# A graph layer and mixture of experts on one core: three sheets for the front of the edge list instead of five, and a ring of 24 gathered tiles in layer 2

## The chip, the cores and the metric

The kernel runs on one core of a Trainium2 chip. The metric is device microseconds of the execution; lower is better. The core has a tensor engine (PE; PEld are its weight loads), a vector engine (DVE), a scalar engine (ACT), GpSimd (POOL) and a sync engine (SP), each with its own instruction stream, and 16 DMA engines.

## What is computed

12500 nodes have 256 features each (x), and 200000 edges (src, dst, weight) are sorted by dst; dst is drawn as 12500 * uniform^2, so low nodes have many more edges. The part that the change touches is `_hconv`, which runs twice:

```
def _hconv(x, src, dst, ew, w1, b1, w2, b2, g, b):
    h = relu(x @ w1 + b1)
    msg = ew[:, None] * h[src]
    agg = segment_sum(msg, dst, num_segments=x.shape[0])
    h = agg @ w2 + b2
    return relu(_bn(h, g, b))
...
x0 = _layernorm(x)
h = relu(_bn(_hconv(x0, layer 1 weights)))
h = _bn(_hconv(h, layer 2 weights))
x = x + relu(h + x0)
x = x + ffn(_layernorm(x))      # 8 experts, all of them for each node, with softmax gates
```

## The kernel before, in words

**Stages.** A prologue (0 to 174 us) makes h of layer 1 and, on DVE, index tables from the edge list. `aggregate(0)` follows (175 to about 1800 us), then batch norms and h1 of layer 2, `aggregate(1)` (1928 to about 3430), and then the last norms and the experts, up to the end of the span.

**Edges.** They are cut into 391 groups of 512, a group into four tiles of 128. There are two ways for a group.

*Gathered groups.* For each tile t POOL issues an indirect DMA (L1054) that fetches 128 rows of h, 1 KB each, by `src_col` into slot t % R of a ring G of R = 16 tiles. The ring has no memory of its own: it lies in buffers that other stages use (`wst`, `f_xr`, `f_u`), so the trace shows these names. PE multiplies the four tiles of a group with four one-hot tiles OH (edge by dst, made by DVE, L1306, a ring of 12 tiles) in 16 matmuls (L1138) into a PSUM tile (`ps` or `px`), and DVE adds this to agg (L1420). Before each tile's first matmul PE waits for that tile's landing, on one semaphore per ring slot (`g_ga0` to `g_ga15`). The last matmul of a group counts `g_mm`, and before it refills four slots POOL waits for the count of the group that used them, four groups back. OH of a group waits for `g_mm` of three groups back.

*Front groups.* The lowest dst have so many edges that the front is done densely. A sheet is a matrix from all source nodes to a few hundred dst columns, made of edges (`MADE`): DVE makes one-hot rows of a tile of edges (`hot_rows`, L1317), ACT their other factor (`lows`, L1203 to L1216), PE multiplies the two (`hot_products`, L1092, tiles hw, ah, al into px) and DVE adds the product to the sheet in the upper part of agg (L1339). A finished segment of a sheet goes to memory by ACT's queue (`front`, L1193) and its place is cleared (L1184, L1225). To use a sheet (`USED`), SP loads it back in blocks (`work<-front`, `work<-h`), and PE multiplies h by it in 98 units (L1106, four matmuls into `pf`, as wide as the sheet), one for each block of 128 source nodes; a DVE add per segment ends it (L1355). Layer 1 makes four sheets (378, 462, 290 and 330 columns; 124 groups) and uses them; layer 2 uses them again, and makes and uses a fifth (416 columns, 16 groups).

So layer 1 gathers 267 groups (1067 tiles; the last group is not full), and layer 2 251 (1003 tiles). Layer 1 runs 496 tiles of edge products and 392 units, layer 2 64 and 490.

**Order.** Nothing is scheduled at run time. A planner at the head of the build places the products, the units and the 25 chunks of z = agg @ w2 (split on ACT L1273, remainder on DVE L1365, PE L1115) behind given groups. In layer 1 products stand behind groups 0 to 188, units behind 30 to 253, z chunks behind 196 to 266; in layer 2 units behind 0 to 229, and z chunks behind 56 to 250, three of them behind group 244 alone. While products run, two of the PSUM tiles serve the gathered groups in turn, and after that four.

Of the kernel before, what the change touches and what calls it, by code (L numbers as in the profile page):

```python
def build(nc, a, out):
# [94 lines left out]
    def sem(name):  # L96
        return top.enter_context(nc.semaphore(name))
# [38 lines left out]
    W_LAST = [SHEET[made[-1]][1] for made in MADE]  # L136
    CLEARS = 4
    A_W = [NHG * HG * max(SHEET[i][1] for i in made) for made in MADE]
# [16 lines left out]
    with top:  # L155
# [581 lines left out]
        R, RO = 16, 12  # L737
        RG, ROG, AG = R // GT, RO // GT, 2
# [3 lines left out]
        ga = [sem(f"g_ga{i}") for i in range(R)]  # L742
# [14 lines left out]
        def gathered_value(layer, t):  # L757

            return 16 * (layer * len(range(t % R, NTL[0], R)) + t // R + 1)
# [158 lines left out]
        def aggregate(layer):  # L918
# [3 lines left out]
            with ExitStack() as s:  # L922
                G = ([w[:, k, :] for w in wst for k in range(KC)] + [xr[:, j, :] for j in range(TPC)]
                     + [u[:, k, i * C:(i + 1) * C] for k in range(KC) for i in range(CH // C)])
                assert len(G) == R
# [8 lines left out]
                def seg_cells(m):  # L934
# [3 lines left out]
                steps = sb(s, f"steps{layer}", [P, WIN_W])[:, :]  # L938

                made_g = range(HOT_G[layer][0], FGL[layer]) if layer else range(FGL[0])  # L940
                ew_parts = sb(s, f"ew_parts{layer}", [P, 2 * GT * len(made_g)])[:, :].rearrange("p (h j f) -> p h j f", h=2, j=GT)
# [6 lines left out]
                    sb(s, f"hw{layer}_{i}", [P, WIN_W], f32r)[:, :] for i in range(2)]  # L948
# [19 lines left out]
                bank_of = [q % 2 if q <= hot_q[layer][-1] else q % 4 for q in range(NQL[layer])]  # L968
# [35 lines left out]
                with nc.Block() as block:  # L1004
                    @block.sync
                    def _(g):
                        if layer == 0:
                            g.wait_ge(window_st, 16 * FB)
                        lo = HOT_G[layer][0] if layer else 0
                        n = GT * (FGL[layer] - lo)  # L1010
                        g.dma_start(window_row[:, 0:n], window_dram[lo:FGL[layer], :].rearrange("(o f) j -> o (f j)", o=1)).then_inc(
                            window_in, 16)
# [35 lines left out]
                    def _(g):  # L1048
                        def gather(t):
                            e = F0[layer] + t  # L1050
                            col = e % GT * TW + e // GT
                            if t % GT == 0 and t >= R:
                                g.wait_ge(g_mm, E0 + t // GT - RG + 1)
                            g.indirect_dma_start(G[t % R], None, h_dram[layer], bass.IndirectOffsetOnAxis(  # L1054
                                ap=src_col[:, col:col + 1], axis=0)).then_inc(ga[t % R], 16)

                        g.iota(steps, pattern=[[1, WIN_W]], base=0, channel_multiplier=0,
                               allow_small_or_imprecise_dtypes=True).then_inc(steps_set, 1)
# [20 lines left out]
                    def _(g):  # L1079
# [48 lines left out]
                        for q in range(NQ):  # L1128
# [3 lines left out]
                            elif q >= 2:  # L1132
                                g.wait_ge(hot_a, H0 + NHOT[layer])
                            for k in range(KC):
                                for t in tiles_of[q]:
                                    if k == 0:
                                        g.wait_ge(ga[t % R], gathered_value(layer, t))
                                    ins = g.matmul(pS[bank_of[q]][:, k, :], G[t % R][:, k * P:(k + 1) * P], OH[t % RO],  # L1138
# [38 lines left out]
                    def _(g):  # L1177
# [42 lines left out]
                        clear(0)  # L1220
                        g.wait_ge(ew_set, 2 * layer + 2)
                        lows(0)
# [3 lines left out]
                        clear(1)  # L1226
# [28 lines left out]
                        for m in (len(made) - 2, len(made) - 1):  # L1255
                            g.wait_ge(hot_f[m % 2], hot_f_value(layer, m))
# [1036 lines left out]
```

## Time and profile before

| | us |
|---|---|
| median of 3 runs | 5256.29 |
| lowest, highest | 5254.63, 5257.71 |
| profiled execution, span | 5228.2 |
| layer 1: first gather to last add | 175.3 to 1796.9 |
| layer 2: first gather to last add | 1928.7 to 3412.5 |

| engine | busy us | share |
|---|---|---|
| PE | 4623.3 | 88% |
| PEld | 3800.6 | 73% |
| DVE | 2688.7 | 51% |
| ACT | 2435.6 | 47% |
| POOL | 2110.6 | 40% |

The profiled execution's own time is given only as its span, from the first to the last instruction; the median is 28 us above it. Shares are over the whole span, in which the experts alone (from about 3430 us) take 1800 us without POOL; the aggregations have to be read by their own stretches. A row of the windows view gives, for a stretch, the busy us and count of each engine in the order PE, PEld, DVE, ACT, POOL, then the granted clock of PE as a share of full speed, the DMA engines' busy share and GB/s. A timeline row gives start, duration, engine, line, operation, tiles, count, and in brackets the idle time ahead of it and what ended it; "issue" is the engine's own pause, "remote" a count that came from elsewhere and that the profile can't put to an instruction.

### The profile page before, as it was taken

Reading aid. Unit: us, or ns where it says so; the run is one execution under the profiler, and the core shown is the slowest. Engines: PE = TensorE matmul, PEld = TensorE weight load, DVE = VectorE, ACT = ScalarE, POOL = GpSimd, SP = SyncE. Lnnn points to the kernel's source line nnn. Section 1 sums busy time; section 2 is a strip of 40 time slices with the busy share of each in tenths; the row PEclk is TensorE's granted clock in tenths of the full one; section 3 lists DMA queues with packets and bytes.
Section 4 is the critical chain, followed back from the end, with each engine's and each line's share of the span. In section 5 each row is a group of like instructions: output and inputs, shape, how many; then the busy total and the mean of one; then the engine's idle time right before and its main releaser. Section 6 shows DMA issues by size and latency. Waiting matters only on the chain. (4 is left out here: it accounts for less than half of the span.)

```text
span 5228.2 us, 71544 instructions
## 1 busy us (share of the span) xinstructions
PE 4623.3 (88%) x25508; PEld 3800.6 (73%) x25508; DVE 2688.7 (51%) x6606; ACT 2435.6 (47%) x4218; POOL 2110.6 (40%) x2284
## 2 busy tenths in 40 slices
PE   6778888888999579888988988649999999999999
PEld 5667777666677467776666666548888888888888
DVE  7666666566333464522222222366666666666665
ACT  4655556666211263300000000057777777777777
POOL 1466666566666456666666666630000000000000
PEclk9889999999999789999999999779999999999999
DMA  5467777566755247876666666431111111001110
GB/s 155 148 210 271 243 240 245 188 211 217 236 198 201 77 141 268 277 243 218 218 219 205 226 212 224 131 96 25 30 28 33 33 33 33 24 26 33 33 28 15
DMA packets 546618, 770.23 MB, mean 147 GB/s; under 512 B 149720, under 2 KB 441411, under 8 KB 546262
## 3 DMA queue, kind: packets, MB, share of 16 engines
q1 hardware_dynamic: 328176, 382.01, 21.7%
q0 software_dynamic: 100944, 273.96, 16.4%
q10 hardware_dynamic: 117142, 109.65, 6.5%
q8 instruction: 206, 3.38, 0.3%
q14 instruction: 150, 1.23, 0.1%
HBM read 605.58 MB, written 147.26 MB: 144 GB/s over the span
## 5 line engine op out<-in xcount | busy, mean ns | idle before, releaser
L1106 PE MATMUL pf<-work 128*128 128x330 f32 (+4 forms) x3528 | 1251.9, 491 | 63.3 <-DMA work<-front 31.3
L1054 POOL DMA_INDIRECT wst<-h,src_col x1040 | 1000.3, 962 | 541.9 <-issue 275.0
L1106 PEld LDWEIGHTS pf<-work 128*128 128x128 f32 x3528 | 661.0, 197 | 402.2 <-issue 220.1
L2096 DVE TENSOR_TENSOR f_hl<-f_hf,f_hh 128x1024 fp32r<-128x1024 f32 (+1 forms) x400 | 479.7, 1199 | 636.3 <-ACT f_hf L1959 636.0
L1952 ACT ACTIVATE f_hh<-f_p,f_sh,f_sc 128x512 fp32r<-128x512 f32 (+1 forms) x800 | 571.7, 768 | 395.9 <-PE f_p L2194 394.5
L1273 ACT ACTIVATE ah<-agg 128x1024 fp32r<-128x1024 f32 (+1 forms) x50 | 51.8, 1037 | 1464.2 <-DVE agg L1420 1086.6
L1138 PEld LDWEIGHTS ps<-oh,wst 128*128 128x128 f32 x4160 | 543.4, 203 | 144.5 <-issue 99.6
L1138 PE MATMUL ps<-oh,wst 128*128 128x128 f32 x4160 | 560.7, 288 | 88.6 <-issue 55.1
L1054 POOL DMA_INDIRECT f_xr<-h,src_col x518 | 497.7, 961 | 282.8 <-issue 134.0
L1054 POOL DMA_INDIRECT f_u<-h,src_col x512 | 491.1, 959 | 260.5 <-issue 136.7
L1959 ACT ACTIVATE f_hf<-f_p,f_sh,f_sc 128x512 f32<-128x512 f32 (+1 forms) x800 | 572.5, 775 | 0.0
L1420 DVE TENSOR_TENSOR agg<-agg,ps 128x68 f32 (+25 forms) x378 | 99.3, 263 | 918.7 <-remote 604.0
L1339 DVE TENSOR_TENSOR agg<-agg,px 128x686 f32 (+5 forms) x560 | 399.3, 713 | 259.4 <-remote 107.7
L1306 DVE TENSOR_SCALAR oh<-lane,rel_col,ew_col 128x36 f32<-128x36 f32 (+27 forms) x2070 | 510.6, 337 | 0.0
L1420 DVE TENSOR_TENSOR agg<-agg,px 128x140 f32 (+20 forms) x140 | 40.5, 289 | 561.5 <-remote 428.6
L2108 DVE SCALAR_TENSOR_TENSOR f_x<-f_p,f_gate,f_x 128x256 f32<-128x256 f32 x784 | 324.4, 476 | 2.4 <-PE f_p L2249 2.4
L2249 PE MATMUL f_p<-Wo_hi,f_hh 128*128 128x256 f32 (+1 forms) x1568 | 317.4, 284 | 2.4 <-DVE f_x L2108 2.4
L2249 PE MATMUL f_p<-Wo_lo,f_hh 128*128 128x256 f32 (+1 forms) x1568 | 314.4, 282 | 0.0
L2249 PE MATMUL f_p<-Wo_hi,f_hl 128*128 128x256 f32 (+1 forms) x1568 | 314.2, 282 | 0.0
L2249 PEld LDWEIGHTS f_p<-Wo_hi,f_hh 128*128 128x128 f32 (+1 forms) x1568 | 250.8, 189 | 25.9 <-issue 11.1
L2194 PE MATMUL f_p<-f_hh,W_hi 128*128 128x512 f32 (+1 forms) x800 | 252.9, 397 | 1.2 <-ACT f_hf L1959 1.2
L2194 PE MATMUL f_p<-f_yh,W_hi 128*128 128x512 f32 (+1 forms) x800 | 248.1, 391 | 4.4 <-DVE f_yl L2047 2.4
(285 smaller groups left out, 7648.0 us busy)
## 6 DMA issues: line engine op xcount, KB each, us to landing
work<-h SPq DMA_DIRECT2D x216, 512.0 KB
work<-front SPq DMA_DIRECT2D x50, 924.0 KB
front<-agg ACTq DMA_DIRECT2D x12, 3300.0 KB
work<-front SPq DMA_DIRECT2D x50, 756.0 KB
work<-front SPq DMA_DIRECT2D x50, 660.0 KB
work<-front SPq DMA_DIRECT2D x50, 580.0 KB
front<-agg ACTq DMA_DIRECT2D x8, 2600.0 KB
work<-front SPq DMA_DIRECT2D x25, 832.0 KB
```

What stands on the lines that cost most here:

```text
L1054: g.indirect_dma_start(G[t % R], None, h_dram[layer], bass.IndirectOffsetOnAxis(ap=src_col[:, col:col + 1], axis=0)).then_inc(ga[t % R], 16)
L1106: ins = g.matmul(pF[:, k, 0:count * w].rearrange("p (s c) -> p s c", c=w), HB[a % 2][0:r, n, k * P:(k + 1) * P], x, start=b == 0, stop=b = ...
L1138: ins = g.matmul(pS[bank_of[q]][:, k, :], G[t % R][:, k * P:(k + 1) * P], OH[t % RO], start=t == tiles_of[q][0], stop=t == tiles_of[q][-1])
L1306: ins = g.tensor_scalar(OH[t % RO][:, 0:wide], lane[:, 0:wide], rel_col[:, col:col + 1], ew_col[:, col:col + 1], ALU.is_equal, ALU.mult)
L1339: g.tensor_tensor(v, v, x, ALU.add).then_inc(hot_a, 1)
L1420: g.tensor_tensor(win, win, pS[bank_of[q]][:, :, 0:wide], ALU.add).then_inc(g_add, 1)
L1952: ins = g.activation(hhi[l][q % 2][:, m, 0:nn], p[:, m, 0:nn], ACT.Relu, bias=shift[l][:, col], scale=scale[l][:, col])
L1959: ins = g.activation(hf[l][:, m, 0:nn], p[:, m, 0:nn], ACT.Relu, bias=shift[l][:, col], scale=scale[l][:, col])
L2096: g.tensor_tensor(hlo[l][q % 2][:, :, 0:nn], hf[l][:, :, 0:nn], hhi[l][q % 2][:, :, 0:nn].bitcast(fp32), ALU.subtract).then_inc(f_lo[l], 1)
L2108: ins = g.scalar_tensor_tensor(X1[0:r, j, :], p3[0:r, j, :], gate[c % 2][0:r, j, e:e + 1], X1[0:r, j, :], ALU.mult, ALU.add)
L2194: ins = g.matmul(o[:, m, 0:nn], ww[:, k, m * P:(m + 1) * P], xx[:, k, 0:nn], start=i == 0 and k == 0, stop=i == 2 and k == KC - 1)
L2249: ins = g.matmul(p3[0:r, j, :], x[:, k, j * P:j * P + r], w[:, k, :], start=n == 0 and k == 0, stop=n == 2 and k == KC - 1)
```

## The change

The front has three sheets instead of five: 378 and 462 columns as before, and a third of 290 columns with 14 groups. Both layers use the same three, 108 groups in all. Layer 1 makes them, layer 2 makes nothing. So 283 groups (1131 tiles) are gathered in both layers; products are 432 tiles in layer 1 (behind groups 0 to 172) and none in layer 2, units 294 in each. With 108 front groups instead of 140, their index tables fit one block of 128 (`FB` is 1 instead of 2). `WIN_W`, the width of the one-hot rows and of the iota ahead of layer 2's gathers, goes from 784 to 688; layer 2 has neither. Its ring gets 8 tiles of memory of their own (`ring1`) behind the 16, so POOL waits for the group six back; layer 1 keeps 16. A semaphore `g_ga` now counts the landings of a group's four tiles together, and PE waits for the four once, ahead of the group's 16 matmuls. In layer 2 four PSUM tiles serve the gathered groups from the start. Units stand behind groups 31 to 268 and z chunks behind 180 to 282 in layer 1, units behind 0 to 226 and z chunks behind 52 to 282 in layer 2, with no three of them behind one group there.

```diff
-               (58, [(5, 3, 7)]),
-               (66, [(5, 3, 7)]),
-               (52, [(2, 2, 7), (6, 2, 8)])]
-    MADE = [[3, 2, 1, 0], [4]]
-    USED = [[3, 2, 1, 0], [3, 2, 1, 0, 4]]
+               (58, [(4, 3, 7), (1, 2, 7)]),
+               ]
+    MADE = [[2, 1, 0], []]
+    USED = [[2, 1, 0], [2, 1, 0]]
...
-    FRONT_C = [3, 4]
+    FRONT_C = [3, 3]
...
-    HOT_Q = [188, 48]
+    HOT_Q = [172, 0]
...
-        R, RO = 16, 12
-        RG, ROG, AG = R // GT, RO // GT, 2
+        R, RO = [16, 24], 12
+        ROG, AG = RO // GT, 2
...
-        ga = [sem(f"g_ga{i}") for i in range(R)]
+        RG = [r // GT for r in R]
+        ga = [sem(f"g_ga{i}") for i in range(max(RG))]
...
-                assert len(G) == R
+                if R[layer] > len(G):
+                    more = sb(s, f"ring{layer}", [P, R[layer] - len(G), C])
+                    G += [more[:, i, :] for i in range(R[layer] - len(G))]
+                ring = R[layer]
...
-                steps = sb(s, f"steps{layer}", [P, WIN_W])[:, :]
+                steps = sb(s, f"steps{layer}", [P, WIN_W])[:, :] if made else None
...
-                bank_of = [q % 2 if q <= hot_q[layer][-1] else q % 4 for q in range(NQL[layer])]
+                bank_of = [q % 2 if made and q <= hot_q[layer][-1] else q % 4 for q in range(NQL[layer])]
...
-                            if t % GT == 0 and t >= R:
-                                g.wait_ge(g_mm, E0 + t // GT - RG + 1)
-                            g.indirect_dma_start(G[t % R], None, h_dram[layer], bass.IndirectOffsetOnAxis(
-                                ap=src_col[:, col:col + 1], axis=0)).then_inc(ga[t % R], 16)
+                            if t % GT == 0 and t >= ring:
+                                g.wait_ge(g_mm, E0 + (t - ring) // GT + 1)
+                            g.indirect_dma_start(G[t % ring], None, h_dram[layer], bass.IndirectOffsetOnAxis(
+                                ap=src_col[:, col:col + 1], axis=0)).then_inc(ga[t // GT % RG[layer]], 16)
...
+                            g.wait_ge(ga[q % RG[layer]], gathered_value(layer, q))
                             for k in range(KC):
                                 for t in tiles_of[q]:
-                                    if k == 0:
-                                        g.wait_ge(ga[t % R], gathered_value(layer, t))
```

POOL, the start of layer 2. Before, an iota stands ahead, and the first wait for `g_mm` comes behind 16 gathers:

```order
L1047 UNCONDITIONAL_BRANCH [waits barrier_Pool_Activation_PE_DVE_SP_gather]
L1057 IOTA steps1 128x784
L1054 DMA wst<-h1,src_col 128x256 x8
L1054 DMA f_xr<-h1,src_col 128x256 x4
L1054 DMA f_u<-h1,src_col 128x256 x4
L1054 DMA wst<-h1,src_col 128x256 [waits g_mm]
L1054 DMA wst<-h1,src_col 128x256 x3
```

The same place after the change:

```order
L1057 UNCONDITIONAL_BRANCH [waits barrier_Pool_Activation_PE_DVE_SP_gather]
L1064 DMA wst<-h1,src_col 128x256 x8
L1064 DMA f_xr<-h1,src_col 128x256 x4
L1064 DMA f_u<-h1,src_col 128x256 x4
L1064 DMA ring1<-h1,src_col 128x256 x8
L1064 DMA wst<-h1,src_col 128x256 [waits g_mm]
L1064 DMA wst<-h1,src_col 128x256 x3
```

Eight more gathers stand ahead of the first wait, and the iota is gone.

PE, layer 1, gathered group 60, before: its matmuls (L1138), then edge products (L1092) and a unit (L1106) of the 330-column sheet:

```order
L1138 MATMUL ps0_0<-oh0,wst 128x128 [waits g_ga0,g_add,g_oh]
L1138 MATMUL ps0_0<-oh0,wst 128x128 [waits g_ga1]
L1138 MATMUL ps0_0<-oh0,wst 128x128 [waits g_ga2]
L1138 MATMUL ps0_0<-oh0,wst 128x128 [waits g_ga3]
L1138 MATMUL ps0_0<-oh0,wst 128x128 x4
L1092 MATMUL px0_1<-ah0_0,ah0_1 128x294 [waits hot_a,hot_m]
L1092 MATMUL px0_1<-ah0_0,ah0_1 128x294 x3
L1106 MATMUL pf0<-work0 128x330 [waits batch_in1]
L1106 MATMUL pf0<-work0 128x330
```

The same group after the change:

```order
L1148 MATMUL ps0_0<-oh0,wst 128x128 [waits g_ga0,g_add,g_oh]
L1148 MATMUL ps0_0<-oh0,wst 128x128 x7
L1103 MATMUL px0_1<-hw0_1,al0 128x294 [waits hot_a,hot_m]
L1103 MATMUL px0_1<-hw0_1,al0 128x294 x3
L1117 MATMUL pf0<-work0 128x290 x2
L1103 MATMUL px0_0<-ah0_0,al0 128x294 [waits hot_a,hot_m]
L1103 MATMUL px0_0<-ah0_0,al0 128x294 x3
```

Four waits for landings became one, and the units are those of the 290-column sheet.

PE, layer 2, gathered group 100, before, with units of the 462-column sheet behind it:

```order
L1138 MATMUL ps1_0<-oh1,wst 128x128 [waits g_ga0,g_add,g_oh]
L1138 MATMUL ps1_0<-oh1,wst 128x128 [waits g_ga1]
L1138 MATMUL ps1_0<-oh1,wst 128x128 [waits g_ga2]
L1138 MATMUL ps1_0<-oh1,wst 128x128 [waits g_ga3]
L1138 MATMUL ps1_0<-oh1,wst 128x128 x4
L1106 MATMUL pf1<-work1 128x462 [waits batch_in1]
L1106 MATMUL pf1<-work1 128x462 x3
```

The same group and the next after the change:

```order
L1148 MATMUL ps1_0<-oh1,ring1 128x128 [waits g_ga4,g_add,g_oh]
L1148 MATMUL ps1_0<-oh1,ring1 128x128 x7
L1117 MATMUL pf1<-work1 128x462 x2
L1148 MATMUL ps1_1<-oh1,ring1 128x128 [waits g_ga5,g_add,g_oh]
L1148 MATMUL ps1_1<-oh1,ring1 128x128 x7
L1117 MATMUL pf1<-work1 128x462 x2
```

Half as many unit matmuls stand between two gathered groups, and the group reads the new tiles of the ring.

## Rows read from the trace of the kernel before

**Rows 1.** Windows: us, PE, PEld, DVE, ACT, POOL busy, clock, DMA share; both aggregations.

```profile
175.00:1338.00 1163.00, 974.52 (x5537) 814.00 (x5538) 726.03 (x1945) 706.98 (x1689) 740.38 (x765) 0.93 0.67 222
1338.00:1779.00 441.00, 396.94 (x2004) 298.59 (x2003) 150.45 (x486) 50.55 (x47) 291.53 (x303) 0.95 0.57 192
1928.00:2243.00 315.00, 274.57 (x1496) 227.75 (x1496) 150.35 (x394) 108.11 (x216) 204.81 (x213) 0.93 0.77 258
2243.00:3397.00 1154.00, 1002.41 (x4926) 737.61 (x4924) 292.70 (x1095) 51.73 (x46) 751.06 (x791) 0.92 0.62 211
```

**Rows 2.** Timeline of POOL in layer 2, about 3300 us.

```profile
3299.36 0.95 POOL L1054 DMA_INDIRECT wst<-h,src_col  x1 [0.30 <-issue]
3303.01 0.95 POOL L1054 DMA_INDIRECT f_xr<-h,src_col  x1 [2.70 <-remote]
```

**Rows 3.** Idle time of POOL ahead of gathers (us, times), layer 1, then layer 2.

```profile
  remote: 174.9, 97
  PE ps L1138: 119.4, 70
...
  issue: 272.2, 892
  remote: 195.6, 90
  PE ps L1138: 28.2, 15
```

**Rows 4.** Timelines of POOL and DVE: iota, last gather and last add of each layer.

```profile
1779.00 0.95 POOL L1054 DMA_INDIRECT f_xr<-h,src_col  x1 [0.30 <-issue]
1796.59 0.33 DVE L1420 TENSOR_TENSOR agg<-agg,px 128x164 f32 x1 [1.01 <-PE px L1138]
1927.80 0.79 POOL L1057 IOTA steps<- 128x784 f32 x1 [9.48 <-POOLq L1570]
1928.74 1.01 POOL L1054 DMA_INDIRECT wst<-h,src_col  x1 [0.16 <-issue]
3396.96 0.95 POOL L1054 DMA_INDIRECT f_xr<-h,src_col  x1 [0.30 <-issue]
3412.15 0.32 DVE L1420 TENSOR_TENSOR agg<-agg,px 128x164 f32 x1 [1.01 <-PE px L1138]
```

**Rows 5.** The page's first line.

```profile
span 5228.2 us, 71544 instructions
```

**Rows 6.** Prologue: the window from 40 to 80 us, and a DVE group by form.

```profile
40.00:80.00 40.00, 22.43 (x106) 19.19 (x107) 36.33 (x148) 14.57 (x26) 0.00 (x0) 0.76 0.35 106
L568 DVE TENSOR_TENSOR agg<-agg,window_f 128x1024 f32<-128x1024 f32 x1 | 1.2, 1219 | 0.0
```

**Rows 7.** Timeline of PE: edge products, a unit of 330, a gathered group, units of 462.

```profile
443.36 0.88 PE L1092 MATMUL px<-hw,ah 128*128 128x344 f32 x4
444.08 1.27 PE L1106 MATMUL pf<-work 128*128 128x330 f32 x4
...
2559.08 3.27 PE L1106 MATMUL pf<-work 128*128 128x462 f32 x8
2562.19 1.95 PE L1138 MATMUL ps<-oh,wst 128*128 128x128 f32 x16
```

**Rows 8.** Timeline of PE at the end of layer 2: z chunks behind group 244.

```profile
3390.88 1.22 PE L1115 MATMUL px<-ah,w_hi 128*128 128x512 f32 x2 [10.77 <-DVE al L1365]
```

**Rows 9.** Windows again: L1106 alone, then all engines in stretches of different load.

```profile
234.00:354.00 120.00, 0.00 (x0) 0.00 (x0) 0.87 0.60 196
...
234.00:354.00 120.00, 86.05 (x505) 77.50 (x504) 76.68 (x187) 73.05 (x154) 78.78 (x82) 0.87 0.60 196
614.00:734.00 120.00, 105.88 (x645) 91.41 (x644) 77.68 (x198) 69.32 (x166) 78.74 (x80) 0.96 0.71 235
1698.00:1758.00 60.00, 50.03 (x274) 40.95 (x273) 19.55 (x69) 3.94 (x4) 40.22 (x43) 0.89 0.42 131
1758.00:1779.00 21.00, 10.51 (x63) 9.06 (x61) 7.39 (x24) 4.26 (x5) 13.35 (x16) 0.76 0.30 89
3290.00:3350.00 60.00, 38.42 (x203) 32.96 (x202) 19.37 (x66) 3.94 (x4) 39.02 (x42) 0.74 0.36 109
```

More of the change, by code:

```diff
@@ L755, in build, with gathered_value, landed @@
         z_out = sem("z_out")
-        def gathered_value(layer, t):
-            return 16 * (layer * len(range(t % R, NTL[0], R)) + t // R + 1)
+        def gathered_value(layer, q):
+            def landed(n, x):
+                return 16 * min(GT, NTL[n] - x * GT)
+            slot = q % RG[layer]
+            before = sum(landed(0, x) for x in range(slot, NQL[0], RG[0])) if layer and slot < RG[0] else 0
+            return before + sum(landed(layer, x) for x in range(slot, q + 1, RG[layer]))
         NFL = [NHG * len(used) for used in USED]
@@ L947, in aggregate @@
                 HW = [AH[0][:, :, :].rearrange("p k n -> p (k n)")[:, 0:WIN_W]] + [
-                    sb(s, f"hw{layer}_{i}", [P, WIN_W], f32r)[:, :] for i in range(2)]
+                    sb(s, f"hw{layer}_{i}", [P, WIN_W], f32r)[:, :] for i in range(2) if made]
                 RH = len(HW)
@@ L1008, in _ @@
                             g.wait_ge(window_st, 16 * FB)
[L1009 to L1012, printed above, removed]
+                        if made:
+                            lo = HOT_G[layer][0] if layer else 0
+                            n = GT * (FGL[layer] - lo)
+                            g.dma_start(window_row[:, 0:n], window_dram[lo:FGL[layer], :].rearrange(
+                                "(o f) j -> o (f j)", o=1)).then_inc(window_in, 16)
                         def load(a):
@@ L1218, in lows @@
                             ins.then_inc(hot_l, 1)
-                        clear(0)
-                        g.wait_ge(ew_set, 2 * layer + 2)
-                        lows(0)
+                        if made:
+                            clear(0)
+                            g.wait_ge(ew_set, 2 * layer + 2)
+                            lows(0)
                         if layer == 0:
@@ L1225, in _ @@
                                 g.activation(agg[:, k, 0:UPPER[0]], zero_col[:, :].broadcast_to([P, UPPER[0]]), ACT.Copy).then_inc(agg_set, 1)
-                        clear(1)
+                        if made:
+                            clear(1)
                         ends = [seg_end(layer, m) for m in range(len(made))]
@@ L1253, in _ @@
                                 store(m)
-                        for m in (len(made) - 2, len(made) - 1):
-                            g.wait_ge(hot_f[m % 2], hot_f_value(layer, m))
-                        g.wait_ge(hot_p, H0 + NHOT[layer])
-                        for k in range(KC):
-                            g.activation(upper[k][:, free_w:], zero_col[:, :].broadcast_to([P, A_W[layer] - free_w]),
-                                         ACT.Copy).then_inc(agg_set, 1)
+                        if made:
+                            for m in (len(made) - 2, len(made) - 1):
+                                g.wait_ge(hot_f[m % 2], hot_f_value(layer, m))
+                            g.wait_ge(hot_p, H0 + NHOT[layer])
+                            for k in range(KC):
+                                g.activation(upper[k][:, free_w:], zero_col[:, :].broadcast_to([P, A_W[layer] - free_w]),
+                                             ACT.Copy).then_inc(agg_set, 1)
                         def split(n):
```

40 lines of the change are left out of this document (22 added, 18 removed).

## The prediction

> **What bounds the kernel now.** I read the stages first: busy time of every engine in four stretches that cover the two aggregations [rows 1]. In none of them is an engine full. TensorE is busy 975 of 1163 us, 397 of 441, 275 of 315 and 1002 of 1154 (84, 90, 87 and 87%); GpSimd, which only gathers, 64 to 66%. But GpSimd's busy time leaves out its issue time. One gather is 0.95 us and then 0.30 us of issue [rows 2], so by the counts of [rows 1] the floor of a group of four tiles is 4 x 1.25 = 5.0 us, and the pace that was reached is 1163 / (765 / 4) = 6.08, 441 / (303 / 4) = 5.82 and, in layer 2, 1469 / 251 = 5.85 us. The rest is waiting, and the second view says for what: GpSimd sat idle for matmuls (remote, and PE ps) for 174.9 + 119.4 us in layer 1 and 195.6 + 28.2 us in layer 2 [rows 3]. Taking off the 0.30 us that each of these 272 gaps would have had anyway leaves about 244 and 192 us. The timeline shows the form: eight gathers back to back, then 2.70 us until a group's matmuls have given its ring slots back [rows 2]. So an aggregation is bound by a loop of gather, landing, matmul, and the ring of 16 tiles (four groups) that closes it, between two engines that are both nearly loaded: GpSimd at 5.0 us a group and TensorE, from [rows 1], at (975 + 397) / 267 = 5.14 in layer 1 and (275 + 1002) / 251 = 5.09 in layer 2. Everything after 3412 us (the last add [rows 4]) and the 130 us between the layers is untouched.
>
> **What the change moves, priced.** The base is the profiled execution, span 5228.2 us [rows 5]; the median of 5256.3 lies 28 us above it, and I add that to the end of every sum, since nothing of the change touches it.
>
> *Prologue.* 108 front groups fit one block of 128 instead of two, so the index work on 128x1024 tiles halves: of five operations at 1.2 us (one is in [rows 6]) half is 3.0 us, and two at 0.7 us, three pairs at 2 x 0.74, 2 x 0.48 and 2 x 0.48 us and small ones bring about 2.8 more, 5.8 us in all. It is on the path in part: VectorE is busy 36.3 of 40 us there [rows 6]. Lost copies, stores and their landings go with it. Taken: -7 us, between -2 and -10.
>
> *TensorE, layer 1.* The removed sheet of 330 columns takes 98 units at 1.27 us = 124 us, and 64 tiles of edge products at 0.72 us (444.08 less 443.36) = 46 us [rows 7]; 16 more gathered groups at 1.95 us cost 31. Net -139: (1372 - 139) / 283 = 4.36 us a group instead of 5.14.
>
> *TensorE, layer 2.* Two sheets leave. The 330 one is 124 us again; the 416 one lies between 330 and 462 columns (1.27 and 3.27 / 2 = 1.64 us), say 1.5, x 98 = 147. Its 64 tiles of products are 46, 32 more groups cost 62. Net -255: (1277 - 255) / 283 = 3.61 us a group. VectorE and ScalarE lose the making too (busy 150 and 108 us of the first 315 [rows 1]); it lay beside GpSimd's work and is worth nothing by itself.
>
> *GpSimd.* Layer 1 has 16 groups more, layer 2 has 32: at the floor 16 x 5.0 = 80 and 160 us of new work on the engine that is now nearest to its own limit.
>
> *Layer 2, ring of 24.* The wait is now for the group six back. The first wait comes at gather 25 instead of 17, and in steady state a slot may be away for 6 x 5.0 = 30 us where 4 x 5.85 = 23.4 us are used now, which is the whole round with its waits in it. TensorE at 3.61 us has room. So I take the floor: 1131 gathers at (204.8 + 751.1) / 1004 + 272.2 / 892 = 0.952 + 0.305 = 1.257 us [rows 1, 3] = 1422 us, plus 10 for leftover waits, plus 16 from last gather to last add (3396.96 to 3412.15 [rows 4]) = 1448, against 3412.5 - 1928.7 = 1484 now: -36. The iota before the first gather (0.79 us [rows 4]) goes: -1. The pile-up at the end, where TensorE waits up to 10.77 us for VectorE's part of three z chunks [rows 8], no longer stands there; no gather waited for it, so it is worth 0. Bounds: -46 (no leftover) and, if the ring gives nothing, 283 x 5.85 + 16 = 1672, +188.
>
> *Layer 1, same ring of 16.* This term decides. At today's paces it would be 172 x 6.08 + 111 x 5.82 + 18 = 1710 us against 1622 (175 to the last add at 1797; 18 is from last gather to last add [rows 4]): +88. At the floor, 1131 x 1.257 + 18 = 1440: -182. What does the pace do when TensorE has less to do? Three rows bear on it [rows 9]. From 234 to 354 us no unit ran (0.00 in the row of L1106), and 82 gathers went out: 5.85 us a group, against 80 (6.0) from 614 to 734 with TensorE 88% busy. From 1698 to 1758, TensorE at 83%, 43 gathers: 5.58; from 1758 to 1779, at 50%, 16 gathers: 5.25. I take 5.9 for the 172 groups beside products (nearest to the unit-free 5.85, since a third of the units is gone) and 5.55 for the 111 behind (nearest to 5.58, the same ring at about the load that all of them will have): 1015 + 616 + 18 = 1649, +27 us.
>
> *Landings per four tiles.* In front of a group's 16 matmuls stands one wait instead of four. It delays the first matmul to the last tile's landing, at most the few matmuls of the first three tiles (under 0.5 us of the 1.95), in the loop of layer 1 only; fewer semaphore instructions stand against it. Taken 0, between -3 and +15 us over layer 1.
>
> *Sum.* -7 + 27 - 36 - 1 = -17: span 5211, time 5239 us, 0.3% faster. It is a small difference of large terms: all but layer 1 brings -44, so the sign turns where layer 1 runs at (1622 + 44 - 18) / 283 = 5.82 us a group over all; today's mean is 6.01, my forecast 5.76.
>
> **Rules of the skill.** On landing: what the rows show is that a slot's round takes 23.4 us in layer 2. The Trainium skill, DMA: Bandwidth & Descriptors, section on the anatomy of one DMA, puts one gather of 128 KB at about 2.0 us plus its bytes over 436 GB/s, so 2.3 us; by that estimate a round is 5.0 + 2.3 + 1.95 = 9.3 us, a ring of 16 would never wait, and the larger ring would be worth nothing. The 224 us of waits decide against it here: most of the round is time behind other work in TensorE's queue and on the way back of the count.
>
> **Rivals.**
> (a) Slower: layer 1's pace stays. For: with no units at all the pace was 5.85, only 0.2 better; from 3290 to 3350 us TensorE was busy 64% and the pace 60 / (42 / 4) = 5.7 [rows 9], so the round of the 16-tile ring looks like latency that an emptier TensorE does not shorten. Against: 5.58 and 5.25 at the end of layer 1. Price: +88 instead of +27, total +44: 5300 us. It decides from 5.82 us a group.
> (b) Slower: layer 2 does not reach GpSimd's floor. The clock is 0.96 while TensorE is 88% busy and 0.74 where it is 64% busy [rows 9]; an emptier TensorE would do its 3.61 us at that clock in 3.61 / 0.74 = 4.9, and with waits the pace could be 5.5: 283 x 5.5 + 16 = 1572, +124 on my layer 2: about 5363. The Trainium skill, TensorE: Matmul & The Clock Gate, Part 1, has the same as a rule: an engine that was idle runs at half clock. The trace agrees (0.74 as a mean of the two levels); the price above is from the rows.
> (c) Faster: two engines near their limits hold each other up, and with TensorE at 4.36 layer 1 follows GpSimd: 283 x 5.4 + 18 = 1546, -76, total -120: 5136 at the end, 5165 at 5.5. For: 5.25 in the last 21 us. Against: 5.85 without units, where TensorE waited for VectorE's adds instead.
>
> **How the numbers follow.** A measurement of this kernel tells 0.2%, 10.5 us, from no change. My forecast 0.46, with its own range 5211 to 5267 from the paces 5.8 to 6.0 and 5.45 to 5.65: 0.32 faster, 0.11 same, 0.03 slower. (a) 0.32: 0.05 same, 0.27 slower. (b) 0.10 slower. (c) 0.12 faster. Together faster 0.44, same 0.16, slower 0.40. The range leaves out the lower half of (c), a little of (a) and most of (b): 5165 to 5312.
>
> **What the profile after would show.** Right: last gather of layer 2 some 1430 us after its first, GpSimd's gaps there 0.30 us almost throughout and no remote idle; layer 1's first 172 groups in about 1015 us and its last 111 in 616; first gather at 168 instead of 175. Wrong on layer 1: 1047 and 646 us with the same remote idle per group as before (0.9 us). Wrong on layer 2: remote idle over 50 us, or clock under 0.8 with TensorE's gather matmuls longer. The forecast falls if layer 1 runs above 5.82 us a group.

## The result: 4.2% slower, and where the time went

The changed kernel takes 5476.32 us (median of 4 runs, 5467.4 to 5482.1) where the kernel before takes 5255.46 us (median of 4 runs, 5250.6 to 5257.7); the ratio is 1.0418, 95% interval 1.0404 to 1.0433. The forecast was 5239 us with a range of 5165 to 5312: wrong in sign, and the result lies 164 us above the range.

Both profiled executions, step by step (a gather's start is the time in its row):

| | before, us | after, us | change |
|---|---|---|---|
| start to layer 1's first gather | 175.3 | 166.4 | -8.9 |
| layer 1, first to last gather | 1603.7 (1067) | 1697.3 (1131) | +93.6 |
| to layer 2's first gather | 149.7 | 140.6 | -9.1 |
| layer 2, first to last gather | 1468.3 (1003) | 1645.1 (1131) | +176.8 |
| to the end of the span | 1831.2 | 1824.3 | -6.9 |
| span | 5228.2 | 5473.7 | +245.5 |

All of the loss lies in the two gathering stretches. The windows of the profile after answer to [rows 1]; the first is layer 1's 172 groups with products, the second its last 111, the third layer 2:

```profile
166.00:1218.00 1052.00, 809.09 (x4558) 687.33 (x4558) 609.48 (x1710) 601.64 (x1459) 669.06 (x690) 0.90 0.59 188
1218.00:1864.00 646.00, 532.63 (x2589) 399.16 (x2587) 199.11 (x670) 55.76 (x61) 420.92 (x443) 0.88 0.51 164
2004.00:3649.00 1645.00, 1243.43 (x5932) 954.93 (x5932) 388.23 (x1515) 45.01 (x46) 1073.47 (x1130) 0.81 0.49 156
```

TensorE's share fell, from 84 to 77% in the first, from 90 to 82% in the second, from 87 to 76% in layer 2, though less than reckoned: it was busy (809 + 533) / 283 = 4.74 and 1243 / 283 = 4.39 us a group, where the prediction had 4.36 and 3.61. The pace did not follow at all: 1052 / 172 = 6.12, 646 / 111 = 5.82 and 1645 / 283 = 5.81 us a group, against 6.08, 5.82 and 5.85 before. Each group that left the sheets was paid at nearly the full old pace: 16 groups in layer 1 cost 94 us (5.85 each), 32 in layer 2 cost 177 us (5.5 each). GpSimd's waits in layer 1, and then in layer 2 with its ring of 24:

```profile
its engine sat idle before it (us, times) until:
  issue: 299.2, 978
  remote: 213.3, 109
  PE ps L1148: 84.2, 39
...
  issue: 318.3, 1036
  remote: 228.9, 83
  PE ps L1148: 14.1, 7
```

Against [rows 3], the waits for matmuls are as long as ever: 298 us in layer 1 instead of 294, 243 in layer 2 instead of 224. In layer 2 only their form changed: between two waits GpSimd now mostly runs twelve gathers (before, eight or twelve), with 96 gaps over 0.5 us instead of 106. The run with a ring of 16 below has 97 such gaps, so even that is not the ring's doing. What held GpSimd was not the ring's length.

### The profile page after: what moved, and what is told of

The parts are those of the page before. It is cut to its first block and busy times, and to the rows that moved or that the text cites. A ratio compares the mean times of both kernels' runs of the same rounds, so it can differ in the third digit from the quotient of the medians.

```text
span 5473.7 us, 68832 instructions
## 1 busy us (share of the span) xinstructions
PE 4546.6 (83%) x24573; PEld 3753.0 (69%) x24573; DVE 2553.6 (47%) x6561; ACT 2216.6 (40%) x3779; POOL 2285.9 (42%) x2471
## 5 line engine op out<-in xcount | busy, mean ns | idle before, releaser
L1064 POOL DMA_INDIRECT wst<-h,src_col x947 | 907.6, 958 | 521.6 <-issue 252.7
L1117 PE MATMUL pf<-work 128*128 128x290 f32 (+2 forms) x2352 | 960.6, 536 | 77.3 <-issue 73.3
L1117 PEld LDWEIGHTS pf<-work 128*128 128x128 f32 x2352 | 467.0, 213 | 326.4 <-issue 242.7
L1435 DVE TENSOR_TENSOR agg<-agg,ps 128x52 f32 (+27 forms) x370 | 95.6, 258 | 1060.4 <-remote 736.2
L1148 PE MATMUL ps<-oh,wst 128*128 128x128 f32 x3040 | 454.7, 301 | 145.3 <-issue 108.9
L1148 PEld LDWEIGHTS ps<-oh,wst 128*128 128x128 f32 x3040 | 431.4, 215 | 194.2 <-issue 177.1
L1319 DVE TENSOR_SCALAR oh<-lane,rel_col,ew_col 128x30 f32<-128x30 f32 (+28 forms) x2262 | 562.5, 338 | 0.2
L1435 DVE TENSOR_TENSOR agg<-agg,px 128x124 f32 (+28 forms) x196 | 53.9, 275 | 898.7 <-remote 713.0
L1064 POOL DMA_INDIRECT ring<-h,src_col x376 | 358.3, 953 | 202.7 <-issue 106.3
L1352 DVE TENSOR_TENSOR agg<-agg,px 128x294 f32 (+4 forms) x432 | 283.3, 656 | 180.0 <-remote 99.3
```

The costliest lines, as they stand in the source:

```text
L1064: g.indirect_dma_start(G[t % ring], None, h_dram[layer], bass.IndirectOffsetOnAxis(ap=src_col[:, col:col + 1], axis=0)).then_inc(ga[t // G ...
L1117: ins = g.matmul(pF[:, k, 0:count * w].rearrange("p (s c) -> p s c", c=w), HB[a % 2][0:r, n, k * P:(k + 1) * P], x, start=b == 0, stop=b = ...
L1148: ins = g.matmul(pS[bank_of[q]][:, k, :], G[t % ring][:, k * P:(k + 1) * P], OH[t % RO], start=t == tiles_of[q][0], stop=t == tiles_of[q][-1])
L1319: ins = g.tensor_scalar(OH[t % RO][:, 0:wide], lane[:, 0:wide], rel_col[:, col:col + 1], ew_col[:, col:col + 1], ALU.is_equal, ALU.mult)
L1352: g.tensor_tensor(v, v, x, ALU.add).then_inc(hot_a, 1)
L1435: g.tensor_tensor(win, win, pS[bank_of[q]][:, :, 0:wide], ALU.add).then_inc(g_add, 1)
```

## The experiments

Each one but the two with four sheets alters layer 2 of the changed kernel alone (layer 1 stays, as a control), and each ran beside a run of the kernel before. One thing has to be said first: the kernel before took 5257.6, 5262.7, 5244.5 and 5252.1 us in four of the five sets, on chips that the record numbers 10, 2, 8 and 4, and 4843.4 us in the remaining set, on chip 3. All kernels of a set share one chip; I call the four the first kind of chip and chip 3 the second. With one chip of it, it can't be told whether the second is a kind or a passing condition. Two kernels are compared within a kind only. The recorded result is of the first.

| kernel | gathers of layer 2 | first to last gather, us | us per gather | total, us |
|---|---|---|---|---|
| changed | 1131 | 1645 | 1.456 | 5476 |
| changed, again | 1131 | 1647 | 1.457 | 5472 |
| ring of 16 | 1131 | 1647 | 1.458 | 5468 |
| a quarter of the units | 1131 | 1638 | 1.450 | 5464 |
| two of four tiles multiplied | 1131 | 1627 | 1.439 | 5445 |
| both, one of four tiles | 1131 | 1607 | 1.422 | 5433 |
| 24 one-hot tiles | 1131 | 1644 | 1.455 | 5467 |
| 64 rows a gather | 1131 | 1652 | 1.462 | 5485 |
| 512 bytes a row | 1131 | 1644 | 1.455 | 5485 |
| three gathers a group | 855 | 1258 | 1.473 | 5086 |
| iota of 64 columns between | 1131 | 1650 | 1.460 | 5488 |
| iota of 264 columns between | 1131 | 1707 | 1.511 | 5536 |
| four sheets, spread | 1067 | 1555 | 1.459 | 5320 |

### What the pace does not depend on

**Ring of 16.** `R, RO = [16, 16], 12`.

> The changed kernel with the ring of layer 2 back at 16 tiles. Layer 2 of the changed kernel took 2004 to 3657 us, 5.8 us a gathered group, with 24 tiles. If the ring's depth matters at all, layer 2 gets longer, to over 5.9 us a group. If something else sets the pace (TensorE's own rate, or the handshake with VectorE over the ring of 12 one-hot tiles), layer 2 stays within 10 us of 1653 us and GpSimd's waits only come every 8 gathers instead of every 12.

Measured 5468.4 us, 1.458 us a gather: eight tiles of ring are worth nothing. The waits still come about every twelfth gather; that they would come every eighth was wrong.

**No gathers.**

```
-                        for t in range(NT_):
+                        for t in range(NT_ if layer == 0 else ring):
                             gather(t)
...
+                            if layer == 0 or q < RG[1]:
                                 g.wait_ge(ga[q % RG[layer]], gathered_value(layer, q))
```

> The changed kernel, but layer 2 issues only the first 24 gathers; all later matmuls read what lies in the ring, so the output is wrong. It leaves out 1107 of 1131 gathers of layer 2 and the waits for their landings. Theory P (the gathers themselves slow TensorE, or bound the pace): a group falls from 5.8 us to about TensorE's own 3.6 to 4.2, layer 2 to 1000 to 1200 us. Theory Q (TensorE and VectorE hold each other up over the one-hot tiles): stays near 5.8 us, 1650 us.

Measured 4791.4 us, 685 less than the changed kernel. The window of layer 2 behind the last gather:

```profile
2026.00:2966.00 940.00, 931.64 (x5854) 769.36 (x5855) 373.50 (x1496) 44.37 (x45) 0.50 (x1) 0.99 0.32 114
```

TensorE is busy 99% of it, and the whole hand-over with VectorE (one-hot tiles, adds) runs at some 3.4 us a group (940 / 276). So the loop of TensorE and VectorE can do far better than 5.8, and it is the gathers that make the pace. Theory Q, that the one-hot ring holds it, falls here.

**Fewer units**, in layer 2 only some 26 of a sheet's 98:

```
-                            for k in range(KC):
+                            for k in range(KC if layer == 0 or b in (0, NB - 1) or b == min((hg + 1) * HG, NB) - 1 else 0):
                                 ins = g.matmul(pF[:, k, 0:count * w]...
```

> The changed kernel, but in layer 2 TensorE runs only some 26 of each sheet's 98 units (first, last and the last of every four), so the output is wrong. Takes about 220 units x 1.4 = 300 us from TensorE, 1.1 us a group. If TensorE's work sets the pace, layer 2 falls from 1653 to 1350 to 1450 us. If GpSimd's gathers or the handshake set it, it stays within 20 us of 1653.

Measured 5463.6 us: TensorE is busy 234 us less in layer 2 (1009 instead of 1243), and that bought 7 us (1.450 us a gather). **Half of the gathered tiles multiplied** (`some = tiles_of[q][:2]` in the matmul loop):

> The changed kernel, but in layer 2 only two of the four gathered tiles of each group are multiplied (8 matmul records a group instead of 16, the output is wrong); all four are gathered and their one-hots made. Takes 0.9 us a group from TensorE by its records. Theory P with a rate limit on GpSimd's side: layer 2 stays at 1653 us. If the gather matmuls themselves are what is slow (they take far longer than the records show): 4.9 us a group or less, down to GpSimd's floor of 5.0, 1430 us.

Measured 5444.6 us, 1.439 us a gather: 19 us less, for 291 us less of TensorE's busy time. Both cuts together, with one tile of four (`tiles_of[q][:1]`):

> The kernel with one tile of four multiplied and a quarter of the units in layer 2, again, to have it on the kind of chip where gathers took 1.45 us. There: 1630 to 1655 us for layer 2's gathers if the rate is the gathers' own; 1420 us if TensorE's share in the loop makes it. On the other kind it repeats 1.255 us a gather.

Measured 5433.5 us, 1.422 us a gather, with TensorE busy 33%:

```profile
2004.00:3610.00 1606.00, 534.75 (x1716) 377.60 (x1716) 382.25 (x1525) 44.99 (x46) 1075.14 (x1130) 0.59 0.50 160
```

That is inconsistent with every theory in which TensorE's amount of work sets the pace, rival (c) of the prediction included: 709 us less of it bought 39 us. It is not quite nothing either; what lets the pace go from 1.456 to 1.422 is left open. **24 one-hot tiles**, `RO, ROG, AG = (12, 3, 2) if layer == 0 else (24, 6, 5)`:

> The changed kernel with 24 one-hot tiles instead of 12 in layer 2, made five groups ahead instead of two. If the hand-over between TensorE and VectorE (one-hot tiles of a group wait for the matmuls of the group three back) sets 5.8 us, layer 2's gathers fall from 1645 us toward 1430. If gathers have a rate of 1.45 us, nothing moves (1640 to 1650 us).

Measured 5467.1 us, 1.455 us a gather: nothing.

### What it does depend on

The light kernel above, and gathers of 64 rows and of 512 bytes a row behind the first 24:

```
+                                g.indirect_dma_start(G[t % ring][0:64, :], None, h_dram[layer], bass.IndirectOffsetOnAxis(
+                                    ap=src_col[0:64, col:col + 1], axis=0))...
...
+                                g.indirect_dma_start(G[t % ring][:, 0:P], None, h_dram[layer].rearrange("n (a c) -> (n a) c", a=2), bass.IndirectOffsetOnAxis(
+                                    ap=src_col[:, col:col + 1], axis=0))...
```

The first runs of these three were on the second kind of chip.

> The changed kernel, but in layer 2 only one of a group's four tiles is multiplied and only some 26 of each sheet's 98 units run (the output is wrong); all gathers stay. TensorE's work falls to about 1.2 us a group. If a group's 5.8 us is a rate of the gathers (1131 gathers at 1.45 us, not the 1.25 us of their issue), layer 2 stays at 1630 to 1655 us. If it is a matter of TensorE and GpSimd holding each other up, it goes to GpSimd's floor, 1430 us.

> The changed kernel, but behind the first 24 the gathers of layer 2 fetch 64 rows instead of 128 (the output is wrong). Half the rows and bytes, the same number of DMAs and of landing counts (16 each). A rate per row or byte: gathers fall from 1.45 us to GpSimd's own time for one (under 1.25 us), layer 2 to at most 1430 us. A rate per DMA or per landing count: stays at 1650 us.

> The changed kernel, but behind the first 24 the gathers of layer 2 fetch 128 rows of 512 bytes instead of 1 KB (the output is wrong). Half the bytes, the same rows, DMAs and counts. A rate per byte: layer 2 falls to 1430 us. A rate per row or per DMA: stays at 1650 us.

Measured 4986.4, 4937.8 and 4986.6 us where the kernel before took 4843.4. Their layer 1 is that of the changed kernel, untouched, and yet it took 1441 us instead of 1697. Idle time of GpSimd in layer 1 of the first of them:

```profile
  issue: 337.5, 1108
  PE ps L1149: 8.9, 20
  PE px L1149: 0.9, 3
```

No remote wait is left. Gathers run at 1.276 us in layer 1, 1.255 in layer 2 and, with 64 rows, 1.211 (its instruction is 0.899 us instead of 0.946): GpSimd's own issue pace, the floor that the prediction reckoned with. So the same program meets that floor on one chip and not on another. These three say nothing of the rate itself, because on this chip GpSimd is the slower part.

They do say what the change is worth where GpSimd's own pace is the limit. The kernels of the first and third have the changed kernel's gathers in number and pace, and they take 4986 us against 4843 before: the change would lose some 143 us there too (an estimate, since the changed kernel itself never ran on this chip).

One more ran there: all 128 indices of a gather the same, which tells of memory.

```
+                            idx = src_col[:, col:col + 1] if layer == 0 else far_idx[:, :]
```

> The changed kernel, but all gathers of layer 2 fetch one and the same row of h 128 times (the output is wrong). If the scattered reads from memory set the rate, layer 2 falls to 1430 us; if GpSimd's descriptors, the DMA path or the counts set it, it stays at 1650 us.

Measured 5693.3 us, 1.851 us a gather, against both expectations. TensorE waits for landings, GpSimd for TensorE:

```profile
  PE ps L1152: 402.2, 62
  issue: 319.0, 1005
  PE px L1152: 296.6, 63
```

Reading one row 128 times is slower than reading 128 scattered rows: the median of one 4 KB DMA packet is 0.73 us instead of 0.16, and a gather's landing takes a median of 23.6 us instead of 2.8. This run is of the second kind, so it doesn't bear on 1.45 us. It has a use as a reference: here GpSimd's 110 waits over 0.5 us at the start of a group all end 0.27 us after the last matmul of the group that held the slots.

The pair was then run on the first kind:

> Gathers of 64 rows in layer 2, again for the same reason. Where a gather took 1.45 us with 128 rows: at most 1.25 us if the rate is per row or byte, 1.45 us if it is per DMA or per landing count. On the other kind of chip it was 1.211 us.

> The kernel with rows of 512 bytes in layer 2, on the kind of chip where 64 rows of 1 KB kept 1.46 us a gather. Rate per DMA: 1.45 us again. Rate per byte or row: 1.25 us.

Measured 1.462 and 1.455 us a gather. Half the rows and half the bytes change nothing; what is left is a cost per DMA, or per something of which each DMA has a fixed number. The kernel with 512 bytes has now run on both kinds, 5484.5 and 4986.6 us; 490 of these 498 us lie between the first and last gathers of the two layers. The next run counts the DMAs, with a semaphore value to match:

```
-                return 16 * min(GT, NTL[n] - x * GT)
+                return 16 * min(GT if n == 0 or x < RG[1] else GT - 1, NTL[n] - x * GT)
...
                         for t in range(NT_):
-                            gather(t)
+                            if layer == 0 or t < ring or t % GT < GT - 1:
+                                gather(t)
```

> The changed kernel, but behind the first 24 gathers layer 2 fetches only three of a group's four tiles (the output is wrong); all four are multiplied. 854 gathers instead of 1131. A rate per DMA of 1.45 us: 4.36 us a group, 1240 us to the last gather. A cost per group: stays at 5.8 us, 1645 us. GpSimd's own pace would be 3.76 us a group and TensorE's 3.6.

Measured 5086.3 us: 855 gathers in 1258 us, 1.473 us each and 4.42 us a group. A gather less takes 1.40 us off a group of 5.82, so the price of a group is that of its gathers, but for some 0.2 us.

### Cause and consequence

The changed kernel's trace shows odd things beside this rate. In places, as here late in layer 2, TensorE's records go out one by one, 0.7 us apart (weight load, matmul, weight load), where the same records run 0.1 us apart elsewhere:

```profile
3447.82 2.38 PE L1148 MATMUL ps<-oh,ring 128*128 128x128 f32 x17
3450.44 0.27 PE L1148 MATMUL ps<-oh,ring 128*128 128x128 f32 x1 [0.23 <-issue]
3451.87 0.27 PE L1148 MATMUL ps<-oh,ring 128*128 128x128 f32 x1 [1.17 <-issue]
...
3461.72 1.44 PE L1148 MATMUL ps<-oh,ring 128*128 128x128 f32 x6 [0.82 <-issue]
```

and the group whose last matmul stands at 3449.4 has its add only 12.6 us later, after a remote wait. The gather that refills this group's slots comes 12.8 us later:

```profile
3462.04 0.31 DVE L1435 TENSOR_TENSOR agg<-agg,ps 128x148 f32 x1 [9.53 <-remote]
3462.18 0.94 POOL L1064 DMA_INDIRECT ring<-h,src_col  x1 [3.44 <-remote]
```

With the light load the same is seen with an idle TensorE. The group of the first row has its last matmul at 2889.9 and its add at 2916.42, 26.5 us later; the group of the second has it at 2900.05, and its add at 2929.16. TensorE meanwhile does nothing for 14.6 us, because it waits for one-hot tiles, which VectorE makes behind the late add.

```profile
2889.33 0.99 PE L1149 MATMUL px<-oh,ring 128*128 128x128 f32 x4 [3.13 <-DMA ring<-h,src_col]
2899.28 1.19 PE L1149 MATMUL ps<-oh,wst 128*128 128x128 f32 x4 [3.87 <-DMA wst<-h,src_col]
2900.27 2.73 PE L1117 MATMUL pf<-work 128*128 128x378 f32 x4
2917.62 1.22 PE L1149 MATMUL px<-oh,f_xr 128*128 128x128 f32 x4 [14.63 <-DVE oh L1320]
...
2916.42 0.27 DVE L1436 TENSOR_TENSOR agg<-agg,px 128x112 f32 x1 [19.06 <-remote]
2929.16 0.27 DVE L1436 TENSOR_TENSOR agg<-agg,ps 128x112 f32 x1 [6.60 <-remote]
```

From the start of a group's last matmul to its add, the mean over layer 2 is 5.6 us in the changed kernel, 10.8 us in this one, 0.6 us without gathers, and 0.54 us for the light kernel on the second kind of chip. GpSimd sees the same: where it had to wait at the start of a group for over 0.5 us, its gather starts a mean of 9.8 us after the last matmul of the group that held the slots (96 cases), where the run with one row fetched 128 times has 0.27. The trace of the kernel before had it already: 4.7 us in layer 2 (106 cases) and 2.6 in layer 1 (161).

The gathers' own transfers are not late. A gather is 32 DMA packets of 4 KB and 16 of 4 bytes, its landing counts. The first packet starts a median of 1.66 us after the gather's row, and the last of the 16 is written a median of 2.45 us after it, at most 6.8, in layer 2 of the changed kernel. The light kernel on the second kind of chip has 1.66, 2.46 and 7.3. So neither the making of a gather's descriptors nor its data is what runs slower on the first kind; what is late there are counts on their way to an engine, and TensorE's records.

Is late counting what slows the gathers, or do gathers that follow each other too closely make the counts late? GpSimd was made to space them:

```
                             gather(t)
+                            if layer == 1:
+                                if t >= 4:
+                                    g.wait_ge(paced, t - 3)
+                                g.iota(pace[:, t % 4, :], pattern=[[1, 64]], base=0, channel_multiplier=0, ...).then_inc(paced, 1)
```

> The changed kernel with a small iota of GpSimd behind every gather of layer 2, which spaces the gathers to about 1.45 us without any wait on TensorE. If 1.45 us is a rate of what the gathers run through, the total stays within 2% of 1645 us (or the iota's own time, if that is longer), GpSimd's waits on TensorE go, and with them the late counts and TensorE's stretches of 0.7 us per instruction. If each gather costs a stall elsewhere, the iotas add 0.2 us each: 1645 + 226 us.

The iota took 0.20 us, but it ate some of the issue gap, so gathers went out every 1.33 us instead of 1.45. Layer 2 came to 1.460 us a gather all the same (5487.9 us), with the missing 0.13 us as waits: in time it did what the first branch said, but the waits did not go, since 1.33 was still too fast. With 264 columns the spacing is 1.51:

> The changed kernel with a longer iota behind every gather of layer 2, so that GpSimd itself issues one every 1.48 to 1.52 us, slower than the 1.455 us that every version reached. If 1.455 us is a rate that something behind the gathers can sustain, the queue never builds up: layer 2 takes 1131 x 1.50 = 1700 us, GpSimd's waits on TensorE nearly vanish (under 20 us instead of 227) and TensorE's instructions 0.7 us apart drop from 430 to under 100. If the stalls come from TensorE whatever GpSimd does, they stay at 0.2 us a gather and layer 2 takes 1900 us.

Measured 5536.4 us, 1707 us for layer 2, and GpSimd's idle time there:

```profile
  issue: 186.3, 1124
  POOLq L1592: 10.1, 1
  PE px L1155: 0.7, 4
  PE ps L1155: 0.3, 2
```

Not one remote wait is left. The mean from last matmul to add falls from 5.6 to 0.46 us, and starts of TensorE's records that lie 0.66 to 0.75 us apart fall from about 450 to 5. With gathers a little slower than 1.455 us, nothing is late and TensorE is quick; with gathers offered faster, the counts are late, the ring fills, and GpSimd is held to 1.455. So the rate of gathers is the cause and TensorE's lateness the consequence. GpSimd offers a gather every 1.253 us, and on this kind of chip something that a gather's landing counts and a matmul's count both pass takes 1.42 to 1.47 us for each gather. That it is the counts is inferred: of what a gather does, the rows, the bytes and the transfers are ruled out, and the 16 counts are what every gather here had.

One rival stands untested. Where counts come late, the trace has also lost most of their records: of the 18096 landing counts of layer 2's gathers, it holds 3695 in the changed kernel, 2234 in the light one and 11615 with the wider iota, and on the second kind of chip 18096 in the light kernel. Every timed execution of the experiments comes with the span and clock of its own trace. Whether writing these records takes part in what is slow, and so whether the 1.455 us would be there in an execution without a trace, no run tells.

### Between the two kernels

Four sheets (124 front groups) in both layers, nothing made in layer 2; the tables as in the kernel before, `MADE = [[3, 2, 1, 0], []]`, `USED = [[3, 2, 1, 0], [3, 2, 1, 0]]`, `HOT_Q = [188, 0]`.

> The changed kernel once more, because the kernel before took 5257 us on the chip of the first four experiments and 4843 us on that of the next four, where layer 1, which none of them alters, ran at 1.276 us a gather with no waits instead of 1.50. On a chip of the first kind: 5476 us again. On one of the second kind both layers run at GpSimd's issue pace (1.276 and 1.255 us a gather): 4985 us, slower than before by 120 to 150 us, as 48 groups more x 5.0 us = 241 less what the emptier TensorE gives back.

The changed kernel itself gave 5472.5 us, on the first kind.

> The changed kernel with before's four sheets of layer 1 (124 front groups, 267 gathered) used in both layers and nothing made in layer 2. Between the two kernels: layer 1 has before's amount of work, layer 2 gathers 16 groups more than before and 16 fewer than the changed one. If each gathered group costs a fixed 5.8 us whatever stands beside it, layer 1 is back at before's 1604 us to the last gather (93 less than the changed one), layer 2 is 16 x 5.8 = 93 us less than the changed one: about 5290 us where before takes 5257. If TensorE's extra units cost time, layer 1 is longer than that. On a chip where a group costs 5.0 us: about 4985 - 160 = 4825 to 4900 us.

Measured 5426.7 us, not 5290: GpSimd has one wait of 124.1 us at the start of layer 2, because the planner put all 98 units of the first sheet used behind group 0 (its room came out at exactly zero, which starts it again at the same group). With the planner's level started at 4020 instead of 4000, it spreads them:

> Four sheets (124 front groups) in both layers, nothing made in layer 2, with the planner's level started at 4020 instead of 4000, which spreads the units that stood behind group 0 in layer 2. Linear price: layer 2's 1067 gathers at 1.455 us = 1552 us (1645 with three sheets, 1468 with before's five), layer 1 as before, 1604 to 1615 us; total 5426 - 122 = 5300 us where before takes 5244 to 5262. On a chip where gathers run at 1.26 us each: 1345 us for layer 2.

Measured 5319.7 us (5252.1 before): 1067 gathers in 1554.9 us, where 1552 was expected, and layer 1 in 1615.6. The total came out at 5320 where 5300 was expected. The price per gather holds between the two kernels. No version with a right output beats the kernel before.

## Why the prediction was wrong, point by point

- **What bounds the kernel.** The reading stopped one step early. That the waits of GpSimd are for matmul counts is in [rows 3] and still true. That they are latency in a loop closed by a ring, which a longer ring or an emptier TensorE shortens, was an interpretation, and the ring of 16, the quarter of the units and the 24 one-hot tiles refute it. The "floor" of 5.0 us a group from [rows 2] was GpSimd's issue, not the rate of what lies behind it. The prediction put most of a slot's round "behind other work in TensorE's queue and on the way back of the count". The second half was right, but it was not sized: the same trace has the waiting gathers of layer 2 start a mean of 4.7 us after the matmuls that they wait for.
- **Layer 2, ring of 24** (taken -36 us, measured +169 from first gather to last add, 1653 against 1484). This is the step that failed most, 205 of the 263 us by which the span was missed: "So I take the floor", 1131 gathers at 1.257 us. They took 1.456 us each, and 1.458 with a ring of 16; in the kernel before they had taken 1.465. The upper bound of the step, 1672 us or +188 "if the ring gives nothing", was the right branch, 19 us off. It had been set aside because 224 us of waits seemed to show that the ring was short.
- **The rule on landing** was set aside for the same reason. By the Trainium skill (DMA: Bandwidth & Descriptors, the anatomy of one DMA) the estimate was 2.3 us for a landing, and so a ring of 16 with room to spare. The trace is near it: where the profile has landings, in layer 2 of the light kernel on the second kind of chip, their median is 2.8 us, and on the first kind the last count of a gather is written after 2.45 us. That a larger ring is worth nothing is what was measured (5468 against 5476 us). That a ring of 16 would never wait holds on the second kind only; on the first GpSimd waits, for counts of matmuls and not for landings.
- **Layer 1** (taken +27, measured +85 from first gather to last add, 1707 against 1622). 172 groups at 5.9 became 6.12, 111 at 5.55 became 5.82: rival (a), whose price of +88 was within 3 us. These are 58 of the 263 us. The row that spoke for it, 5.85 us with no unit at all [rows 9], was the one to trust; the 21 us at 5.25 were too short, 16 gathers, to carry a term.
- **Rival (a)** took layer 1 right but kept layer 2 at its floor, so it gave 5300. Had I let one cause act in both layers, the working would have been -7 + 88 + 188 - 1 = +268 against the spans' +245.5. The two terms were treated as independent, and they share their cause.
- **Rival (b)** foresaw a slower layer 2, at 5.5 us a group, by the clock. The clock did fall, from 0.93 over layer 2 to 0.81, but it is no cause: at 0.59, in the light kernel, the pace was slightly better.
- **Prologue** (taken -7): -8.9. **Iota** (-1): the stretch from layer 1's last gather to layer 2's first is 9.1 us shorter; 8.2 us of it lie ahead of layer 1's last add, which now comes 9.7 us after the last gather instead of 17.9. Layer 2's tail is shorter in the same way, 7.9 us where 16 were taken. **Landings per four tiles** (0): no run separates it.
- **28 us around the span.** I added the difference between the median and the profiled span of before as if it were fixed. In all later runs the two are 1.8 to 2.0 us apart. The profiled execution of before was a quick one, and by its span the change costs 245 us where the medians say 221.

## What to carry to other kernels

When an engine waits for another in a ring, look first at how long after the other's instruction each wait ends: 0.27 us where nothing is in the way here, 4.7 us in the kernel before. Another test is whether the waits go when the other engine gets less to do; a stretch of the profile without that work, at the same pace, has already made it. Where pace stays the same in stretches of very different load, look for a rate of the one thing that all of them have in common, here the indirect DMA, and price work by the number of those, not by the issue time. And if one cause might explain waits in two stages, move it in both at once when bounding the sum.

## What the runs showed of the hardware

- On four chips an indirect gather could be sustained every 1.42 to 1.47 us in layer 2 (1.49 to 1.52 in layer 1), whether of 128 or 64 rows, of 1 KB or 512 bytes; on a fifth at least every 1.255 us, or 1.211 with 64 rows. The kernel before takes 8.5% longer on the four (5255 against 4843 us). All of this is from executions that were traced.
- Offered faster than that rate, gathers delay other engines: the add that waits for a group's matmuls comes up to 20 us after the last of them in the changed kernel and up to 30 us in the light one, and TensorE's records go out 0.7 us apart. The gathers' own packets are not delayed (first packet after 1.66 us, last count written after 2.45 us, medians, as on the fifth chip). What takes the time is left open: each gather has 16 landing counts, but no run changed that number, and none ran without a trace.
- Gathering one row 128 times took 1.851 us a gather where scattered rows took 1.255 (both on the fifth chip), with 0.73 us a packet of 4 KB instead of 0.16.
- The last matmul of a group stands in the record at 3449.4, and what waits for its count starts at 3462.0 (VectorE) and 3462.2 (GpSimd); so the start of a TensorE record doesn't say when a result was ready. The Trainium skill (Perfetto Trace Analysis, Tensor Engine Instruction) puts the reported start at the begin of the data read and calls the end an estimate; these rows don't tell whether the matmuls themselves ran late or only their counts.
